# Both halves of an expert tile scattered into one table, one at a time, in a small language model's mixture-of-experts layers

## The reference

```python
x = layernorm(h)
g = top_k(x @ Wg + bg, k)              # k = 1 of 4 in layer 0, k = 2 of 8 in layer 1
y[e] = act(x @ W1[e] + b1[e]) @ W2[e] + b2[e]
h = h + sum_i weight_i * y[g_i]        # one term in layer 0, two in layer 1
```

## Time and profile before

| what | value |
|---|---|
| median of three runs | 1828.41 us |
| profiled execution, its own time | 1812.08 us |
| its span, first to last instruction | 1810.3 us |
| layer 0's expert tiles, first to last scatter's start | 1207.69 to 1288.15 us |
| layer 1's expert tiles, first to last scatter's start | 1597.80 to 1775.88 us |

### The profile page before, as it was taken

The page is one execution under the profiler, slowest core; times in us unless marked ns, Lnnn a source line. Parts: engine busy times, 40 slices in busy tenths (PEclk is TensorE's granted clock), DMA queues, the critical chain, the costliest instruction groups (busy, mean ns, idle before and its releaser), DMA issues.

```text
span 1810.3 us, 39511 instructions
## 1 busy us (share of the span) xinstructions
PE 1452.2 (80%) x13098; PEld 1219.3 (67%) x13098; DVE 1240.0 (68%) x3514; ACT 979.3 (54%) x2393; POOL 815.8 (45%) x1175
## 2 busy tenths in 40 slices
PE   2688798898898888988879488569478887499991
PEld 1577677776776766867768478269457666399991
DVE  6888877888678797688887722434478896434444
ACT  1588535886337884358862133245258882155550
POOL 7786235762347742368623200135365511145540
PEclk9899999999999999999999787679779996599996
DMA  4644005470026430075610000167345501367766
GB/s 114 164 98 96 1 1 133 96 140 14 1 47 160 98 78 1 6 175 107 180 55 1 14 1 1 48 202 243 121 97 120 102 2 47 110 191 237 243 201 182
DMA packets 144278, 177.87 MB, mean 98 GB/s; under 512 B 22096, under 2 KB 106128, under 8 KB 143952
## 3 DMA queue, kind: packets, MB, share of 16 engines
q1 hardware_dynamic: 136784, 158.18, 34.3%
q0 software_dynamic: 7296, 17.18, 2.8%
HBM read 132.96 MB, written 42.34 MB: 97 GB/s over the span
## 4 chain that ended last, share of the span: by engine, by line
PE 51%; DVE 26%; issue 9%; POOL 6%; DMA 3%; ACT 3%; SPq 1%; DVEq 0%; POOLq 0%; ACTq 0%
PE bank L1480 7%; DVE ptl L804 7%; PE bank L646 7%; DVE neg_max L797 4%; PE bank L558 3%; PE bank L426 2%; PE bank L1466 2%; PE bank L444 2%; PE bank L579 2%; PE bank L445 2%; PE bank L446 2%; PE bank L448 2%; PE bank L447 2%; DVE xx L771 2%; DVE au L827 1%
## 5 line engine op out<-in xcount | busy, mean ns | idle before, releaser
L686 ACT ACTIVATE prob<-bank,neg_max 128x192 f32<-128x192 f32 (+1 forms) x960 | 408.8, 437 | 131.6 <-DVE neg_max L797 119.5
L797 DVE TENSOR_REDUCE neg_max<-bank 128x2 f32<-128x384 f32 (+1 forms) x480 | 272.7, 570 | 82.3 <-PE bank L539 81.5
L804 DVE TENSOR_TENSOR ptl<-bank,pth 128x384 f16<-128x384 f32 (+1 forms) x480 | 274.5, 572 | 9.4 <-ACT pth L699 8.7
L558 PE MATMUL bank<-ident,prob 128*128 128x128 f32 x1536 | 266.4, 286 | 0.0
L699 ACT ACTIVATE pth<-bank 128x384 f16<-128x384 f32 (+1 forms) x480 | 244.7, 510 | 6.5 <-PE bank L558 6.0
L653 ACT ACTIVATE xx<-bank 128x256 fp32r<-128x256 f32 x256 | 95.5, 387 | 176.2 <-PE bank L426 172.9
L539 PE MATMUL bank<-kx,qx 96*128 96x192 bf16 (+1 forms) x960 | 166.8, 255 | 1.1 <-DVE xx L771 1.1
L558 PEld LDWEIGHTS bank<-ident,prob 128*128 128x128 f32 x1536 | 161.5, 142 | 0.0
L579 PE MATMUL bank<-v,pth 128*128 128x33 bf16 x1152 | 137.9, 179 | 21.5 <-DVE ptl L804 18.5
L737 ACT ACTIVATE fbuf<-bank,b 128x512 f32<-128x512 f32 x96 | 65.9, 687 | 162.7 <-PE bank L448 162.7
L646 PE MATMUL bank<-w,fbuf 128*128 128x192 f32 x768 | 140.7, 326 | 1.9 <-DVE h L896 1.9
(11 more groups left out here) (297 smaller groups left out, 4491.6 us busy)
## 6 DMA issues: line engine op xcount, KB each, us to landing
xn<-in_e_seg SPq DMA_DIRECT2D x34, 768.0 KB, 6.7
w<-in_e_w SPq DMA_DIRECT2D x23, 576.0 KB, 4.0
qk_rows<-fbuf SPq DMA_DIRECT2D x128, 96.0 KB, 2.3
qx<-qk_rows SPq DMA_DIRECT2D x35, 288.0 KB, 4.1
kx<-qk_rows SPq DMA_DIRECT2D x35, 288.0 KB, 5.9
qk_rows<-w SPq DMA_DIRECT2D x80, 96.0 KB, 2.3
qx<-qk_rows SPq DMA_DIRECT2D x35, 192.0 KB, 4.6
kx<-qk_rows SPq DMA_DIRECT2D x35, 192.0 KB, 5.3
```

The source lines that it names most:

```text
L558: last = nc.tensor.transpose(bank[BT[p % 2]][:, c * P:c * P + P], probs_at(p, banded, c * P, P), ident[:, :])
L686: nc.scalar.activation(probs_at(p, banded, qt * n, n), scores_at(p, n)[:, qt, :], ACT.Exp, bias=neg_max[:, b % 2, hd, qt:qt + 1], scale=1. ...
L797: nc.vector.tensor_reduce(neg_max[:, b % 2, hd, :], scores_at(p, D if banded else S), AX.X, ALU.max, negate=True).then_inc(max_ready.sem, 1)
L804: nc.vector.tensor_tensor(ptl[:, p % 2, 0:n], bank[BT[p % 2]][:, 0:n], pth[:, p % 3, 0:n], ALU.subtract)\
```

## The change

There is one table `y_rows` in place of two. Each scatter now waits for the scatter issued just before it, whichever half that was: half 1 of a tile for half 0 of that tile, half 0 for half 1 of the tile before. In POOL's loop the scatter of half 0 moves in front of the two gathers of the tile three later, and the scatter of half 1 stays behind them. SP reads one table back, so half as many loads, and none waits for VectorE. The merge (`copy_predicated`, the mask `d_odd`, the signal `merged`, the buffers `odd_sums`) is gone, and VectorE adds from the loaded rows at once. The first fill writes one table.

```diff
@@ sp_sums, dve_merge
-            y = [r[0:NT * P * PICKS[m], :].rearrange("(t p) d -> p t d", p=P) for r in y_rows]
+            y = y_rows[0:NT * P * PICKS[m], :].rearrange("(t p) d -> p t d", p=P)
             for s in range(2):
                 sp.wait_ge(e_sent[s].sem, 16 * (span(m)[-1] + 1))
             for g in range(NG):
-                if g >= 2:
-                    sp.wait_ge(merged.sem, merged.at(m, g - 1))
                 for k in range(PICKS[m]):
                     tg, tk = slice(GT * g, GT * g + GT), slice(k * NT + GT * g, k * NT + GT * g + GT)
-                    sp.dma_start(sums(k)[:, tg, :], y[0][:, tk, :]).then_inc(sums_in[g].sem, 16)
-                    sp.dma_start(odd_sums(m, g, k), y[1][:, tk, :]).then_inc(sums_in[g].sem, 16)
-
-        def dve_merge(dve, ch, m, g):
-
-            dve.wait_ge(sums_in[g].sem, 32 * (PICKS[m] if m == 0 else PICKS[0] + PICKS[1]))
-            for k in range(PICKS[m]):
-                tg, tk = slice(GT * g, GT * g + GT), slice(k * NT + GT * g, k * NT + GT * g + GT)
-                ch.mark(nc.vector.copy_predicated(sums(k)[:, tg, :], d_odd[:, tk].unsqueeze(2).to_broadcast([P, GT, D]),
-                                                  odd_sums(m, g, k)))
-            ch.done(ch.n)
-            dve.sem_inc(merged.sem, 1)
+                    sp.dma_start(sums(k)[:, tg, :], y[:, tk, :]).then_inc(sums_in[g].sem, 16)
+
+        def dve_sums(dve, m, g):
+
+            dve.wait_ge(sums_in[g].sem, 16 * (PICKS[m] if m == 0 else PICKS[0] + PICKS[1]))
@@ put and POOL's loop in pool_tiles
                 pool.wait_ge(e_y_ready.sem, 2 * G + s + 1)
-                if G > 0:
-                    pool.wait_ge(e_sent[s].sem, 16 * G)
+                if G + s > 0:
+                    pool.wait_ge(e_sent[1 - s].sem, 16 * (G + s))
                 i = 2 * (G - first) + s
-                pool.indirect_dma_start(out=y_rows[s], in_=vf[:, 2 * (G % 2) + s, :], in_offset=None,
+                pool.indirect_dma_start(out=y_rows, in_=vf[:, 2 * (G % 2) + s, :], in_offset=None,
...
             for G in range(first, end + 1):
+                if G > first:
+                    put(G - 1, 0)
                 for s in range(2):
                     if G + 2 < end:
                         get(G + 2, s)
-                for s in range(2):
-                    if G > first:
-                        put(G - 1, s)
+                if G > first:
+                    put(G - 1, 1)
@@ dve_places
-            ch.mark(v.tensor_scalar(d_odd[:, 0:b], d_pos_i[:, 0:b], P, None, ALU.bitwise_and))
@@ the first fill
-            for s in range(2):
-                for i in range(4):
-                    sp.dma_start(y_rows[s][8 * P * i:8 * P * (i + 1), :].rearrange("(t p) d -> p t d", p=P), filler)\
-                        .then_inc(filled.sem, 16)
+            for i in range(4):
+                sp.dma_start(y_rows[8 * P * i:8 * P * (i + 1), :].rearrange("(t p) d -> p t d", p=P), filler)\
+                    .then_inc(filled.sem, 16)
@@ layer 0's use of the sums on VectorE; in layer 1 dve_merge(dve, ch, 1, g) became dve_sums(dve, 1, g)
+            added = {}
             for g in range(NG + 2):
                 if g < NG:
                     tg = slice(GT * g, GT * g + GT)
-                    dve_merge(dve, ch, 0, g)
-                    added = ch.mark(nc.vector.tensor_tensor(h[:, tg, 0:D], h[:, tg, 0:D], hb[:, tg, :], ALU.add))
+                    dve_sums(dve, 0, g)
+                    added[g] = ch.mark(nc.vector.tensor_tensor(h[:, tg, 0:D], h[:, tg, 0:D], hb[:, tg, :], ALU.add))
                 if g == NG:
-                    ch.done(added)
+                    ch.done(added[NG - 1])
                     dve.sem_inc(sum_ready.sem, 1)
                 if 1 <= g <= NG:
+                    ch.done(added[g - 1])
                     dve_stats(dve, ch, L + 1, 0, g - 1, None)
```

More of the change, by code:

```diff
@@ L222, in build_tower @@
         d_mul = part(128)
-        d_pos, d_div, d_pos_i, d_mod, d_odd = part(32), part(32), part(32, I32), part(32, I32), part(32, I32)
+        d_pos, d_div, d_pos_i, d_mod = part(32), part(32), part(32, I32), part(32, I32)
         d_many, d_more = part(8), part(64, dims="p (e j) -> p e j", e=8)
@@ L327, in build_tower @@
         e_sent = [sig(f"e_sent_{s}", base=0) for s in range(2)]
-        merged = sig("merged", per=NG, base=0)
         filled = sig("filled", base=0)
@@ L342, in build_tower @@
         x_rows = nc.dram_tensor("x_rows", (NT * P, 256), F32, kind="Internal").ap()
-        y_rows = [nc.dram_tensor(f"y_rows_{s}", ((2 * NT + 1) * P, D), F32, kind="Internal").ap() for s in range(2)]
+        y_rows = nc.dram_tensor("y_rows", ((2 * NT + 1) * P, D), F32, kind="Internal").ap()
         qk_rows = [nc.dram_tensor(f"qk_rows_{j}", (2, 2, 3, 3 * DH, 4 * S), BF16, kind="Internal").ap() for j in range(2)]
@@ L1318, in build_tower @@
                           .rearrange("p (t d) -> p t d", d=D))[k]
-        odd_sums = lambda m, g, k: spare[:, NT * 256 + ((2 * (g % 2) + k) - 4 if m else g % 2 - 2) * GT * D:][:, 0:GT * D]\
-            .rearrange("p (t d) -> p t d", d=D)
         marks = lambda m: chosen[:, 0:(NT + 1) * EXPERTS[m]].rearrange("p (t e) -> p t e", e=EXPERTS[m])
@@ L1697, in _ @@
                 sp.dma_start(dst, src).then_inc(aux_in.sem, 16)
-            sp.wait_ge(filled.sem, 16 * 8)
+            sp.wait_ge(filled.sem, 16 * 4)
             sp.dma_start(d_lists, a["lists"]).then_inc(lists_in.sem, 16)
@@ L2063, in _ @@
             for g in range(NG):
-                dve_merge(dve, ch, 1, g)
+                dve_sums(dve, 1, g)
                 for k in range(2):
```

## The result

| kernel | median us | runs | ratio, 95% interval |
|---|---|---|---|
| before | 1828.24 | 4 | |
| changed | 1887.44 | 4 | 1.0326 [1.0294, 1.0357] |

The change makes the kernel 59 us slower, where 22 were forecast. The profiled execution took 1882.14 us, its span is 1880.3. Against the span before, this is 70 us more; 12.6 of them lie ahead of the first gather of layer 0 (at 1194.16 us, before at 1181.60), where the two programs differ only by the first fill and one mask instruction.

A forecast was written before the change was run, and what follows sets the result against it. PE's matmuls were taken to bound the tiles at 8.13 us. Cadence +37.0, tails +2.0, end of program -11.3 and layer 0 -6.0 sum to +21.7 us, giving 1850 us on the median, range 1822 to 1878.

The forecast's parts named there:

- the cadence: Expert tiles, both layers: second scatter starts at 3.9 us and lands 5.7 later; 9.5 against 8.13 us over 27 tiles, +37.0 us.
- The first half: Tile's first scatter: gets away before the big loads and lands in about 4.3 us; second scatter taken to start at 3.9.
- The third rival: Expert tiles: both halves fall behind the loads, cadence up to 13; at 11.5 us, +76 us, so 1904 us; chance 0.10.
- its reason against: Third rival, expert tiles: loads wait for VectorE's output, so they slow down with the chain and cannot overtake it.
- Number of tiles: Tiles that pay the longer cadence: 19 in layer 1 and 8 of 11 in layer 0, 27 together.
- Tails at the end of each mixture: Last scatters of each mixture: the second waits 2.3 us for the first's landing, where it followed after 1.3; +2.0 us.
- End of the program: Layer 1's read-back: merges gone and half the loads, so VectorE ends at 1795.9 instead of 1807.2; -11.3 us.
- Layer 0, -6.0: Layer 0's read-back: statistics start 4.4 us earlier, and 1.6 us more from two further merges gone; -6.0 us.
- slack of 1 us: Expert tiles: gathers moved behind the next tile's first scatter land about 1 us before PE's transposes need them.
- I count nothing for it: Expert tiles: PE's clock might fall below 1.00 when its busy share goes to 0.86; no cost counted.
- The first rival: Expert tiles: serial chain hidden, cadence stays 8.13 if second scatters land within 4.2 us; -15.3 us, so 1813; chance 0.11.

The follow-up runs named there:

- waits_swapped: Changed kernel with the two waits ahead of a scatter swapped, the scatter before first, then VectorE's output; 1860.82 us, ratio 1.0185.
- chain_only: Kernel before with one edit: each scatter waits for the one issued just before it; two tables, gathers first and merges kept; 1892.15 us, ratio 1.0380.
- light_loads: Changed kernel, but from each mixture's fourth tile on both matrix loads fetch only 8 columns; 1810.00 us, ratio 0.9921.
- half_chain: Kernel before with the new loop order; half 1 also waits for its tile's half 0, half 0 only for a scatter one tile back; 1829.97 us, ratio 1.0038.
- before_b2: Kernel before, with the expert's second bias held once per partition in the input instead of one row read 128 times; 1823.37 us, ratio 0.9995.

## Why the prediction was wrong

The direction and the mechanism held. PE bounded the tiles, POOL's scatters became the bound at once, PE stalls at the transposes for late gathers, and matrix loads make the landings long.

**The step that failed** is the cadence, the time from one tile's first scatter to the next tile's: "3.9 + 5.7 = 9.6, at most 3.9 + 6.5 = 10.4", of which 9.5 was taken. Measured: 10.91 in layer 1, and 10.77 over layer 0's first 8 tiles (1219.30 to 1305.46). Over the 27 tiles (19 at +2.78, 8 at +2.64) the term is +74 where +37 was forecast. In layer 1 the first link, from a tile's first scatter to its second, takes 5.3 us in the mean where 3.9 were counted, and that is the whole miss (5.0 in layer 0). The second link takes 5.6 us, as counted (5.8 in layer 0), but by luck: its landing is 4.7 us in the mean where 5.7 were taken, and the step behind it, which nobody counted, makes up for it. What was left out:

- The step from a landing to the next scatter. The prediction counted none. It is 0.78 us wherever a scatter waits for a landing; made 0.3, the kernel is 26.6 us faster (waits_swapped), and the 27 tiles are 0.55 us shorter each in the traces, of the 1.37 us per tile that the forecast missed. Even the trace before shows it once: a scatter waited there for another and started 0.8 us after its landing (1723.47 + 5.7, then 1729.96), and I passed it over.
- The first half. The prediction let the second scatter start at 3.9, although it read that first halves land in 4.3 us. By its own reading the second could not start before 4.3, and with the step not before 5.1, which is nearly the 5.3 measured. The 4.3 itself holds only while the first half starts ahead of the loads. In the chain it starts where the scatter before it has landed, wherever the loads are then, and lands in 2.3 to 6.9 us, 4.1 in the mean. The third rival, "both halves fall behind the loads", was true in part, in a milder form than the 11.5 us at which it was priced: in 6 of the 19 tiles both halves take over 4 us. The loads did slow down with the chain, as its reason against says: the share of the DMA engines fell from 0.77 to 0.59. Landings still ranged from 2.3 to 7.0 us.

**The other terms.** Number of tiles: 27 held. Tails at the end of each mixture, +2.0: each is now 3.1 us between the last two scatters (1854.17 and 1857.25), before 1.3, so +3.6 in these pairs. But the whole stretch behind the 8 and the 19 tiles grew by 3.2 us in layer 0 (18.56 from 15.41) and shrank by 0.5 in layer 1 (23.01 from 23.54), +2.6 together: the pairs were undersized by the same step, the term comes out near its forecast. End of the program, -11.3: measured -11.4. Layer 0, -6.0: the statistics come 4.6 us earlier behind the last scatter, and the first gather of layer 1 4.9 us (282.6 us behind the last scatter of layer 0, before 287.4). Sum of the parts in the trace: the stretch from first gather to last scatter +23.3 in layer 0 and +50.4 in layer 1, then -4.9 and -11.4: +57.4, against 59.2 of the medians. These differ from the sum of the terms by the first scatters, which start 1.0 and 1.9 us earlier behind the first gather of their layer. The order of the gathers was costed at nothing with a slack of 1 us; without the chain it costs 7 us, beside it the cost isn't clear.

**The clock.** "I count nothing for it" was the text on a PE clock below 1.00. It is 0.90 in these tiles, a mean of stretches at 1.00 and of lower ones behind PE's waits: PE waited 8.23 us for a gather until 1661.50, and from 1662.48 to 1670.18 the granted clock is 0.77. That isn't what makes them long: in chain_only the granted clock over layer 0's first 8 tiles is 0.98, and a tile still takes 10.58 us.

```profile
1222.77:1307.39 84.62, 73.56 (x509) 69.77 (x508) 29.65 (x69) 42.12 (x88) 31.69 (x31) 0.98 0.59 179
```

What the clock adds can be bounded from the landings of the changed kernel (an estimate): if each of the 38 links of layer 1's 19 tiles took its landing and 0.78 us, and a first link at least the 3.85 us of the two gathers, they would sum to 202.1 of the 207.36 us. Only the other 5.2 us can be scatters that waited for VectorE's output beyond that, and so for a slower PE.

**The first rival**, that the serial chain is hidden, needed landings under 4.2 us. light_loads gives it these, and the chain is hidden indeed.

## What to carry to other kernels

When two transfers that ran side by side are put in a row, price the closed cycle: the sum of all landings and of all steps from a landing to the next issue, against the time of one round; here half of the cycle cost nothing (half_chain), and the whole of it 68 us (chain_only). Take the landing from rows with the load that will lie beside it at each place that the chain can drift to, not from where the transfer sits now. Where an instruction waits for two things, write the one that comes last in both orders and measure.

## What the runs showed of the hardware that was not expected

- The order of two waits ahead of one indirect DMA on POOL moves its start by 0.5 us: 0.8 us after a landing with the wait on VectorE's output written first, 0.3 with it written last (waits_swapped, 26.6 us over the kernel).
- A load of 96 KB that reads one 768-byte row for 128 partitions holds up what is behind it: reading 128 rows instead shortened scatters' landings from 6.5 to 5.6 us (before_b2) and gave 13.6 us where scatters were the bound.
- The part ahead of layer 0's tiles, nearly the same in all of these kernels, differed by up to 16.6 us between their profiled executions. The four that had the first gather by 1184 us show a granted clock of 0.87 over 800 to 1180 us, the other nine, which had it from 1191 us on, 0.84 to 0.86. No run here tells why.
